# Eight transposes put between wide matmuls, and a residual add put ahead of a subtraction, in a graph layer on one core

## What is computed

```python
agg = segment_sum(x[src], dst)
mean = agg / maximum(deg, 1)
h = mean @ W_l + b + x @ W_r
x = layernorm(x + h * sigmoid(h))
```

## Time and profile before

| | |
|---|---|
| three runs, median | 1676.12 us (1675.56 to 1676.58) |
| the profiled execution's own time | 1675.46 us |
| its span, first to last instruction | 1673.6 us |
| TensorE matmul busy | 1607.3 us, 96% |
| TensorE weight load busy | 1315.8 us, 79% |
| VectorE busy | 1446.7 us, 86% |
| ScalarE busy | 972.1 us, 58% |
| GpSimd busy | 1014.5 us, 61% |
| mean granted clock of TensorE | 0.993 of full speed |

### The profile page before, as it was taken

The page is one execution under the profiler, slowest core; times in us unless marked ns, Lnnn a source line. Parts: engine busy times, 40 slices in busy tenths (PEclk is TensorE's granted clock), DMA queues, the critical chain, the costliest instruction groups (busy, mean ns, idle before and its releaser), DMA issues.

```text
span 1673.6 us, 30193 instructions
## 1 busy us (share of the span) xinstructions
PE 1607.3 (96%) x7886; PEld 1315.8 (79%) x7886; DVE 1446.7 (86%) x2468; ACT 972.1 (58%) x1237; POOL 1014.5 (61%) x1306
## 2 busy tenths in 40 slices
PE   7998999999999999999999999999999999999995
PEld 5887777777777788888878888887888888888884
DVE  8889999999997788888888888888888888888886
ACT  4443111111113677777767777776777777777775
POOL 5445555555553666666666666665666666666664
PEclk9999999999999999999999999999999999999998
DMA  5455788888885566666666666766666666666664
GB/s 181 150 163 173 211 238 235 238 235 236 238 233 176 159 211 224 207 218 212 211 206 217 206 223 202 224 206 200 226 198 228 203 223 211 216 207 213 209 218 162
DMA packets 204143, 349.25 MB, mean 209 GB/s; under 512 B 37020, under 2 KB 51126, under 8 KB 204117
## 3 DMA queue, kind: packets, MB, share of 16 engines
q1 hardware_dynamic: 156135, 274.22, 49.4%
q0 software_dynamic: 46944, 74.22, 17.1%
q10 hardware_dynamic: 1038, 0.50, 0.1%
HBM read 288.78 MB, written 139.67 MB: 256 GB/s over the span
## 4 chain that ended last, share of the span: by engine, by line
issue 30%; PE 20%; POOL 19%; DVE 17%; ACT 10%; POOLq 2%; DVEq 1%; DMA 1%; ACTq 0%; SPq 0%
PE pH L490 17%; POOL cor L391 6%; ACT O L703 4%; DVE Z L975 4%; DVE stats L990 3%; POOL rstd L462 3%; POOL light_cor L391 3%; ACT cor L666 2%; DVE sums L911 2%; POOL l_var_eps L442 2%; POOL var_eps L459 2%; ACT light_o L720 2%; DVE l_stats L1017 2%; POOL l_rstd L444 1%; ACT s_hi L660 1%
## 5 line engine op out<-in xcount | busy, mean ns | idle before, releaser
L490 PE MATMUL pH<-ws_hi,x_hi 128*128 128x512 f32 x1564 | 631.5, 404 | 13.6 <-DVE x_lo L962 6.7
L490 PE MATMUL pH<-ws_hi,x_lo 128*128 128x512 f32 x1564 | 613.3, 392 | 0.0
L490 PE MATMUL pH<-ws_lo,x_hi 128*128 128x512 f32 x1564 | 611.1, 391 | 0.0
L391 POOL DMA_INDIRECT cor<-correction_rows,node_now x347 | 370.8, 1069 | 215.4 <-POOL node_now L423 148.4
L490 PEld LDWEIGHTS pH<-ws_hi,x_hi 128*128 128x128 f32 x1564 | 295.1, 189 | 77.4 <-issue 22.7
L490 PEld LDWEIGHTS pH<-ws_hi,x_lo 128*128 128x128 f32 x1564 | 294.5, 188 | 64.5
L711 ACT ACTIVATE Z<-Z 128x1024 f32<-128x1024 f32 x174 | 184.2, 1058 | 272.2 <-DVE Z L975 236.0
L490 PEld LDWEIGHTS pH<-ws_lo,x_hi 128*128 128x128 f32 x1564 | 295.9, 189 | 55.2
L703 ACT ACTIVATE O<-Z,shift,rstd 128x512 f32<-128x512 f32 x347 | 261.5, 801 | 3.7 <-DVE shift L1001 3.7
L975 DVE TENSOR_TENSOR Z<-pH,cor 128x1024 f32<-128x1024 f32 x174 | 212.0, 1218 | 27.3 <-issue 15.2
L660 ACT ACTIVATE s_hi<-sums 128x512 fp32r<-128x512 f32 x98 | 62.0, 632 | 287.8 <-DVE sums L911 177.4
(11 more groups left out here) (131 smaller groups left out, 1789.7 us busy)
## 6 DMA issues: line engine op xcount, KB each, us to landing
X<-in_x SPq DMA_DIRECT2D x173, 512.0 KB
out<-O SPq DMA_DIRECT2D x173, 512.0 KB
correction_rows<-c_out SPq DMA_DIRECT2D x98, 256.0 KB
light_x<-in_x SPq DMA_DIRECT2D x66, 256.0 KB
light_h<-early_product SPq DMA_DIRECT2D x44, 256.0 KB
out<-light_o SPq DMA_DIRECT2D x44, 256.0 KB
join_row<-joined SPq DMA_DIRECT2D x98, 64.0 KB
light_h<-in_x SPq DMA_DIRECT2D x22, 256.0 KB, 2.7
```

The lines of the kernel that those rows point to most:

```text
L391: g.indirect_dma_start(out=out_, out_offset=None, in_=table, in_offset=bass.IndirectOffsetOnAxis(ap=idx, axis=0), bounds_check=bound, oob_ ...
L490: last = mm(ps, a[:, k], w[:, k], start=(n == 0), stop=(n == len(terms) - 1))
```

## The change

TensorE issues no block of eight transposes ahead of a pair's wide matmuls any more. It issues one of the eight transposes of pair t+1 behind each of the first eight wide matmuls of pair t. The wait for `X` of pair t+1 stays ahead of the wide matmuls; the wait for `x_lo` of t-1 goes, since `x_lo` of t is waited for at the same place. The function `three` is written out in place. In VectorE's order `residual` of t-1 comes ahead of `split_x` of t+1. The orders of ScalarE, SP and GpSimd are as before.

```diff
             def node_pair(t, q, u):
-                shifted(t, q, u, 1, NP, transpose_x)
                 nt, rows = pair_shape(t)
                 b = u % 2
                 wait(pe, hi_made, t + 1)
...
                 wait(pe, z_made, t - 1)
+                if not fixed(t) or t + 1 < NP:
+                    next_b, used = ring(q + (u + 1) // 4, (u + 1) % 4, 4)
+                    next_nt, next_rows = pair_shape(t + 1)
+                    blocks = next_nt * K
+                    pe.wait_ge(x_in[next_b], 16 * (used + 1))
+                    if fixed(t) and t < 1:
+                        pe.wait_ge(sums_made, ET)
+                else:
+                    blocks = 0
                 for a in range(nt):
-                    last = three(pH[b][0:rows, a, :], x_hi[b][:, a, :, 0:rows], x_lo[b][:, a, :, 0:rows],
-                                 ws_hi, ws_lo)
+                    n = 0
+                    for k in range(K):
+                        for x_part, w_part in ((x_hi, ws_hi), (x_hi, ws_lo), (x_lo, ws_hi)):
+                            last = mm(pH[b][0:rows, a, :], x_part[b][:, a, k, 0:rows], w_part[:, k],
+                                      start=(n == 0), stop=(n == 3 * K - 1))
+                            if a == 0 and n < blocks:
+                                to, i = divmod(n, K)
+                                turned_x = nc.tensor.transpose(pT[1 - b][:, to, i * P:i * P + next_rows],
+                                                               X[0:next_rows, next_b, to, i * P:(i + 1) * P],
+                                                               eye[0:next_rows, 0:next_rows])
+                                if n == blocks - 1:
+                                    turned_x.then_inc(transposed, 1)
+                            n += 1
                 last.then_inc(product, 1)
...
             def node_pair(t, q, u):
                 shifted(t, q, u, -1, NP, add_cor)
                 shifted(t, q, u, -2, NP, moments)
+                shifted(t, q, u, -1, NP, residual)
                 shifted(t, q, u, 1, NP, split_x)
-                shifted(t, q, u, -1, NP, residual)
                 shifted(t, q, u, -2, NP, make_shift)
                 light(q, u)
```

## The result

The changed kernel takes 1863.88 us (median of 4 runs, 1862.82 to 1867.62) against 1675.84 us for the kernel before in the same set: a ratio of 1.1125, 95% interval 1.1111 to 1.1139. The profiled execution took 1864.06 us, with a span of 1862.2 us.

The account below looks back on a forecast made before the run. TensorE bounds the kernel before; after the change, a closed chain of waits through three engines does. 1675.46 us plus 167 × (7.465 − 6.471) = 166, less 0.5 at start and end, gives 1841 us; range 1758 to 1885.

Parts of the forecast that it names:

- the closed circle: Node stage: wide matmuls, transposes, x_hi, silu, residual, x_lo, next wide matmuls wait in turn; 7.465 us a pair, 74%.
- the last hand-off: From x_lo's end on VectorE to TensorE's next first wide matmul: 0.11 us.
- The last one starts at 2.69: TensorE: the last of the eight transposes starts 2.69 us after the pair's wide matmuls begin.
- the hand-off to x_hi: From the end of the last transpose on TensorE to the start of x_hi on ScalarE: 0.04 us.
- Nothing won there: TensorE's own work: alternating transposes cost 0.11 us each, as in the block, so its sum gains nothing.
- loads are hidden: TensorE rival: wide matmuls cover transposes' weight loads, each transpose costing 0 to 0.11 us; 1768 us at half, 14%.
- alternation is dear: TensorE rival: each alternating transpose costs up to 0.34 us; up to 2149 us, halfway 1995 us, 5%.
- The start and the end: Outside the 167 periods: first five pairs +1 us, end −1.5 us, together −0.5 us.
- The drain: End of the stage: VectorE is less behind, so Z can start at once; −1.5 us.
- The clock falls: TensorE rival: idle time lowers the clock from 2.4 to 1.2 GHz; 11.2 us a pair, 2465 us, 2%.
- The circle doesn't close: ScalarE rival: silu of t−1 done before x_hi of t+1, so TensorE stays the bound; 6.35 us a pair, 1655 us, 4%.
- the 6.43 of the prediction's own sum: TensorE's own time a pair with alternation: 0.08 + 24 × 0.228 + 8 × 0.11 = 6.43 us.

Follow-up runs that it names:

- the run with waits of 2.5 us: Changed kernel with one transpose behind every second wide matmul instead of behind each of the first eight: 2362.77 us (one run).
- the unhindered alternation: Changed kernel with silu ahead of x_hi on ScalarE, shift behind the next Z on VectorE, and TensorE's wait for X first: 1674.07 us, ratio 0.9976.

## Why the prediction was right, and where it was off

- **Direction and mechanism: right.** It named the closed circle (wide matmuls, transposes, x_hi, silu, residual, x_lo) from the order of three engines, and the timeline shows its six steps in that order without a gap. That both halves are needed, that taking silu out opens it, and that moving the last transpose by 0.95 us moves the time by 150 us are shown by the runs.
- **Size: 7.611 us a pair in place of 7.465,** 24 us over 167 pairs; nearly all of the difference between 1841 and 1864 us. No single term carries it; the biggest part is the last hand-off. "The wide matmuls start 0.11 later" measured 0.18 in the mean of pairs 12 to 169 (0.10 in two of four pairs, 0.19 and 0.33 in the others): 0.07 more. "The last one starts at 2.69" measured 2.74, with 0.346 for a wide matmul and a transpose in place of 0.34. x_hi, x_lo and the hand-off to x_hi together are 0.06 longer (x_hi 1.03 against 1.01 and x_lo 1.22 against 1.195), silu and its overlap 0.03 shorter. The hand-off was taken from one row, without asking whether all four steps of the loop have it. The ends of the range carry small slips: give or take 47 us around 1841 is 1794 to 1888, and a transpose at 0.05 us gives 1761; neither matters to the outcome.
- **"Nothing won there" for TensorE: right.** 0.34 us for a wide matmul and a transpose, from the block's spacing, held to 0.01. No row of before showed an alternation, so the price was borrowed from the nearest row and not worked out; that it held so closely was in part luck. The rivals "loads are hidden" and "alternation is dear" both fall with it. By the 56 ns that the prediction takes from the Trainium skill ("TensorE: Matmul & The Clock Gate", Part 2, back-to-back issue gap) the two would take about 0.28 us together, an estimate; 0.346 was measured.
- **The start and the end:** pair 5 starts 0.3 us earlier, but not because of the change: pair 0 had started 2.5 us earlier (525.48, before 527.93), behind stages that the change leaves alone. From the start of pair 0 to that of pair 5 the changed kernel takes 2.1 us more (forecast +1). The drain came to −1.4 us (forecast −1.5).
- **"The clock falls": not here, and the reason given is borne out.** Waits of 0.9 us left it alone. In the run with waits of 2.5 us it fell.
- **"The circle doesn't close": its condition was right, its price wrong.** With silu ahead of x_hi the time is 1683 and not 1655 us. That rival took TensorE's 6.35 us with the block of transposes, though it kept the alternation; the 6.43 of the prediction's own sum would have been the one to take (the median pair of the unhindered alternation took 6.46). Part of the rest was waits elsewhere: with shift and the wait for X moved too, 1683 became 1674 us.
- **What the prediction missed:** the VectorE edit was priced only inside the circle. Alone it is worth −23 us, because it takes residual away from GpSimd's rstd. The 0.12 us between 6.35 and 6.47 were put down to VectorE coming next; that it was VectorE waiting for rstd, and that the order of two operations decides it, was in the trace and was not read.

## What to carry to other kernels

Before a step is moved, write down for one period what each engine does in its written order and look for a closed path through all of them: its length is a bound that no engine's busy share shows. Two edits that are each harmless can close such a path together, so try them apart. And read the waits of the second busiest engine as closely as those of the first: a wait of 0.6 us in one pair of four was worth more here than the edit on the engine that was full.

## What the runs showed of the hardware that was not expected

**VectorE's add of two SBUF operands holds up small GpSimd operations.** In the kernel before, rstd (two values in each of 128 partitions) takes 0.72 us beside x_lo, which reads PSUM and SBUF, and up to 1.83 us when it meets residual, which reads SBUF twice; it then ends after residual, by 0.57 to 0.59 us in all 43 cases. Between 600 and 1600 us, 75 rstd began beside x_lo and 41 beside nothing on VectorE, all at 0.72 to 0.73 us; the 38 that began beside residual took 1.68 to 1.80. Its mean is 986 ns there and 723 with the other order (no rstd over 733), while var_eps, which residual then meets, rises from 257 to 613. The Trainium skill ("SBUF — State Buffer", Who interferes with whom) has the rule: a VectorE operation with both inputs in SBUF contends with GpSimd's reads. The traces agree. The other form of the add with the same operands (986 ns again) shows that it isn't the form of the operation, which points to where its inputs lie; a residual with one operand elsewhere was not tried.

**A falling clock costs time even where TensorE is not full.** With TensorE idle for 2.5 of some 9 us, its slow matmuls still cost 1.7 us a pair in the mean (10.9 in place of 9.2), since the transposes among them are on the circle.

**The same wait costs 0.10 to 0.33 us after its end,** by what is written behind it; with the wait that ends last put last it was 0.145 us in every step of the loop.
